# The last tiles of a graph gather cut into groups of 3, 2, 2 and 2 in place of 4, 3 and 2

## The chip, the cores and the metric

One core of one Trainium2 chip. The metric is the device time of one execution in microseconds (us), the median of several executions. Every execution does the whole computation once.

## The reference

The program is a small network on 6250 nodes with 256 features and 100000 edges sorted by destination. It has four layers, each added to its input: a graph layer that takes the mean over a node's neighbours, a mixture of eight experts of which each node takes two, a graph attention layer, and a second, smaller mixture. The change lies in the first layer and in the choice of experts of the second:

```python
x = x + _L0_gnn_ref(_layernorm(x, axis=-1), edge_index, L0_gnn_W, L0_gnn_b)
x = x + _L0_ffn_ref(_layernorm(x, axis=-1)[None], L0_ffn_Wg, ...)[0]
x = x + _L1_gnn_ref(_layernorm(x, axis=-1), edge_index, L1_gnn_W, L1_gnn_a_src, L1_gnn_a_dst)
x = x + _L1_ffn_ref(_layernorm(x, axis=-1)[None], L1_ffn_sW1, ...)[0]

# _L0_gnn_ref
neigh_sum = jax.ops.segment_sum(input_matrix[src], dst, num_segments=N_NODES)
neigh_mean = neigh_sum / jnp.maximum(deg, 1.0)[:, None]
out = jax.nn.relu(jnp.concatenate([input_matrix, neigh_mean], axis=-1) @ W + b)
return out / jnp.maximum(jnp.linalg.norm(out, axis=-1, keepdims=True), EPS)

# _L0_ffn_ref, the choice
gate_scores = jnp.einsum('bsd,ed->bse', x, Wg) + bg
topk_scores, topk_idx = jax.lax.top_k(gate_scores, K)
```

## The kernel before

Nodes lie in 49 tiles of 128 (`NT`; the last has 106 real nodes). Edges lie in 98 supers of 1024 (`NS`), each fetched by eight indirect DMAs of 128 rows that GpSimd issues one after the other (`gather_supers`, L699) into a ring of seven supers (`R0`); SyncE counts a super as landed at L851. A node tile's neighbour sum is made of items, one item for each pair of a super and a tile that meet in it: 146 in all (`ITEMS`). For an item VectorE builds a one-hot matrix (L712), TensorE multiplies it with the eight gathered blocks (L864), and VectorE adds the result to the tile's row of `ACC` (L1051).

The tiles are cut into groups by `GROUPS` (L43), and the work goes in rounds, an order that is written out by hand on each engine. Round r does the items of group r and then a tail in which four groups stand at four stages:

- group r (called new): divide by the degree (L1138, L1121), turn the rows (L876, L878), and the dense layer (L887, L889), with ScalarE copying and applying the relu (L963, L967, L973);
- group r-1 (mid): scale to unit length, add to `X` (L1125), moments (L1130, L196 to L204), normalise (L214), turn (L914) and the scores of the experts (L923);
- group r-2: on VectorE the best two experts (`choose`, L1060 to L1073), on TensorE their ranks (L904, L905), on VectorE the places in the experts' lists (`positions`, L1080 to L1101);
- group r-3 (old): tile by tile on VectorE three rows of hots for each of two choices (`list_hots`, L1110 to L1114), and on TensorE four products that write them into the lists (`to_lists`, L895).

So there are as many rounds as groups plus three (`LAGS`). TensorE and VectorE go through items and tail in program order, so no item is multiplied while a tail runs. The gather goes on beside it, as far as the ring lets it. VectorE's tail of a round:

```python
if new:
    ...
    tile_in(new[0], 0)
    tile_in(new[1], 1)
if 0 <= r - 2 < NG:
    choose(r - 2)
...
for n in range(max(len(new), steps, len(old))):
    if 2 <= n < len(new):
        tile_in(new[n], n)
    for t in mid[2 * n:2 * n + 2]:
        new_x(t)
    if n < len(old):
        list_hots(old[n], r - 3)
```

Items are taken in pairs, and the first pair of a group is read from a table that the kernel makes of the sorted edges (`tile_pair`, `group_span`). A third or fourth tile of a group enters its tail inside the loop, behind the hots of earlier steps. When the last round is over, all engines meet, and the experts' layer begins with the reading of the counts (L1241).

Of the kernel before, what the change touches and what calls it, by code (L numbers as in the profile page):

```python
# [27 lines left out]
class Sizes:  # L28


    def __init__(self, n_nodes, d, n_edges, n_exp, hid, heads):
        self.N, self.D, self.E = n_nodes, d, n_edges
        self.NT = -(-n_nodes // P)
        self.NPAD = self.NT * P
        self.KD = d // P
        self.Q = 8
        self.SE = self.Q * P
        self.NS = -(-n_edges // self.SE)
        self.RG = -(-self.NS * self.Q // P)
        self.EPAD = (self.RG * P + 1) * P  # L40
        self.R = 8
        self.R0 = 7
        self.GROUPS = (4,) * 11 + (3, 2)  # L43
        self.ECOLS = self.NT + self.NT % 2
        self.ITEMS = self.NS + self.NT - 1
        self.TABW = self.ITEMS + 4
        self.SRANGE = self.NS + 4
        self.BS = 2
        self.NB = self.NS // self.BS
        self.NE, self.HID = n_exp, hid  # L50
        self.KH = hid // P
        self.HEADS = heads
        self.TOK = 256
        self.ET = (2 * self.NPAD + n_exp * (self.TOK - 1)) // self.TOK
        self.LEAST = n_nodes * 2 // (8 * self.TOK) * 8
        self.NEVER = 8191
        assert self.ITEMS % 2 == 0 and self.NS % self.BS == 0 and self.R == 4 * self.BS and self.NB > 4
        assert self.NT % 2 and self.NEVER >= self.NPAD
        assert sum(self.GROUPS) == self.NT and min(self.GROUPS) >= 2 and self.NS % self.R0 == 0
        assert n_exp * self.ECOLS <= 512 and 2 * self.NT < 256  # L60
# [2417 lines left out]
```

How the kernel before makes its waits and increments, by code:

```python
    def settle(self):  # L73
        self.eng.wait_ge(self.sem, self.n)
# [110 lines left out]
        def ln_root(act, s_var, s_root):  # L185
            act.wait_ge(s_var, 1)
            nc.scalar.activation(lnt[:, 2], lnt[:, 0], ACT.Sqrt).then_inc(s_root, 1)
# [1 line left out]
        def ln_rstd(loc, s_root):  # L189
            loc.eng.wait_ge(s_root, 1)
            loc.link(nc.vector.reciprocal(rstd[:], lnt[:, 2]))
# [60 lines left out]
            def rows_ready(loc, s_rows, s_rowsf):  # L252
                loc.eng.wait_ge(s_rows, 16 * len(LISTS))
                loc.link(nc.vector.tensor_copy(rows_f[:], rows_i[:]))
                loc.link(nc.vector.tensor_tensor(rows_i[:, 0], rows_f[:, 1], rows_f[:, 2], ALU.is_gt))
# [16 lines left out]
            def store_gaps(sp, s_rowsf, s_gaps):  # L274
                sp.wait_ge(s_rowsf, 2)
                for n, to in enumerate((seg_gaps, gaps_back)):
                    sp.dma_start(to.rearrange("(g p e) -> p g e", p=P, e=P), gaps[:, n]).then_inc(s_gaps, 16)
                sp.wait_ge(s_gaps, 32)
# [1 line left out]
            def turn_lists(pe, s_rowsf, s_turned, s_copied):  # L280
                pe.wait_ge(s_rowsf, 1)
                for t in range(NTURN):
                    n, g = divmod(t, z.RG)
                    if t >= 2:
                        pe.wait_ge(s_copied, t - 1)
                    nc.tensor.matmul(pT[t % 2][:, 0:P], rows_f[:, n, g, :], front[:], start=True, stop=False)
                    nc.tensor.matmul(pT[t % 2][:, 0:P], rows_b[:, n, g, :], back[:], start=False, stop=True)\
                        .then_inc(s_turned, 1)
```

## Time and profile before

| what | before |
|---|---|
| median of 3 runs | 3563.06 us (3559.85 to 3564.49) |
| the profiled execution's own time | 3562.46 us |
| its span | 3560.7 us |
| first gather, GpSimd's DMAs | 103.6 to 1093.9 us of the span |
| tail of the last group begins (L1138) | 1119.6 us |
| next stage begins (L1241) | 1175.5 us |
| VectorE, TensorE busy | 50%, 78% |

The span runs from the first instruction to the last; the execution's own time is 1.8 us longer. Times in the trace's views are us from the span's start. A row of the timeline has start, length, engine, line, operation, the tiles written and read, how many instructions it merges, and in brackets how long the engine sat idle before it and for whom. PE is TensorE (PEld its weight loads), DVE VectorE, ACT ScalarE, POOL GpSimd, SP SyncE.

### The profile page before, as it was taken

Reading aid. Unit: us, or ns where it says so; the run is one execution under the profiler, and the core shown is the slowest. Engines: PE = TensorE matmul, PEld = TensorE weight load, DVE = VectorE, ACT = ScalarE, POOL = GpSimd, SP = SyncE. Lnnn points to the kernel's source line nnn. Section 1 sums busy time; section 2 is a strip of 40 time slices with the busy share of each in tenths; the row PEclk is TensorE's granted clock in tenths of the full one; section 3 lists DMA queues with packets and bytes.
Section 4 is the critical chain, followed back from the end, with each engine's and each line's share of the span. In section 5 each row is a group of like instructions: output and inputs, shape, how many; then the busy total and the mean of one; then the engine's idle time right before and its main releaser. Section 6 shows DMA issues by size and latency. Waiting matters only on the chain. (4 is left out here: it accounts for less than half of the span.)

```text
span 3560.7 us, 54707 instructions
## 1 busy us (share of the span) xinstructions
PE 2771.3 (78%) x12865; PEld 2282.5 (64%) x12866; DVE 1767.8 (50%) x4610; ACT 1149.8 (32%) x4236; POOL 1718.6 (48%) x1811
## 2 busy tenths in 40 slices
PE   1477778788887699999999445777777767768999
PEld 1356666666665488888888334555555555558888
DVE  5323455444456311111111656777777777766664
ACT  2000101000001122222222226556656556534554
POOL 0677777777772122222222037777777777500000
PEclk7688888888897799999999777888888887888999
DMA  4433333333331122212221544444444444300000
GB/s 148 124 105 111 110 109 110 114 112 109 110 110 46 71 85 81 91 60 89 100 70 59 159 123 112 110 109 110 110 110 109 110 110 110 86 23 14 17 19 21
DMA packets 157662, 328.30 MB, mean 92 GB/s; under 512 B 40129, under 2 KB 95323, under 8 KB 153356
## 3 DMA queue, kind: packets, MB, share of 16 engines
q0 software_dynamic: 85824, 236.38, 23.7%
q1 hardware_dynamic: 58816, 77.11, 6.4%
q10 hardware_dynamic: 12844, 12.82, 1.1%
q8 instruction: 65, 1.06, 0.1%
q14 instruction: 113, 0.93, 0.1%
HBM read 286.42 MB, written 41.86 MB: 92 GB/s over the span
## 5 line engine op out<-in xcount | busy, mean ns | idle before, releaser
L699 POOL DMA_INDIRECT G<-g_rows,srcT x784 | 742.3, 947 | 368.3 <-issue 236.7
L699 POOL DMA_INDIRECT G<-h_rows,srcT x784 | 752.8, 960 | 238.8 <-issue 237.6
L864 PE MATMUL pS<-G,O 128*128 x2336 | 565.9, 406 | 168.4 <-issue 98.2
L1789 PE MATMUL pS<-G,O 128*128 x2336 | 653.2, 446 | 37.5 <-issue 29.0
L864 PEld LDWEIGHTS pS<-G,O 128*128 128x128 f32 x2336 | 473.9, 205 | 256.8 <-issue 178.9
L1789 PEld LDWEIGHTS pS<-G,O 128*128 128x128 f32 x2336 | 507.0, 220 | 184.5 <-issue 59.1
L1858 ACT ACTIVATE G<-G 128x32 f32<-128x32 f32 x2352 | 503.1, 307 | 0.0
L1433 ACT ACTIVATE HE<-pH,b1s 128x256 f32<-128x256 f32 x432 | 204.9, 474 | 583.8 <-PE pH L1408 583.8
L1408 PE MATMUL pH<-XT,w1s 128*128 128x256 f32 x1728 | 384.5, 381 | 0.9 <-DVE XT L1448 0.9
L1418 PE MATMUL pY<-w2s,HE 128*128 128x256 f32 x1728 | 381.9, 379 | 0.0
L1340 POOL DMA_INDIRECT y_rows<-YE,yidx x108 | 109.3, 1012 | 527.7 <-DVE YE L1460 511.3
L1408 PEld LDWEIGHTS pH<-XT,w1s 128*128 128x128 f32 x1728 | 330.1, 191 | 46.6 <-issue 1.3
L1418 PEld LDWEIGHTS pY<-w2s,HE 128*128 128x128 f32 x1728 | 324.1, 190 | 41.8
L963 ACT ACTIVATE HT<-pT 128x512 f32<-128x512 f32 x49 | 29.2, 596 | 825.6 <-PE pT L878 825.5
L1799 PE MATMUL pA<-ident,SCO 128*64 128x128 f32 x196 | 52.0, 421 | 287.0 <-ACT SCO L1840 287.0
L1947 DVE SCALAR_TENSOR_TENSOR O<-iota_bank,tile_base,dstT 128x1024 f32<-128x1024 f32 x146 | 187.4, 1284 | 170.2 <-PE pS L1789 121.7
L712 DVE SCALAR_TENSOR_TENSOR O<-iota_bank,tile_base,dstT 128x1024 f32<-128x1024 f32 x149 | 191.2, 1284 | 130.8 <-issue 129.8
L1051 DVE TENSOR_TENSOR ACC<-ACC,pS 128x257 f32 x146 | 62.0, 424 | 318.8 <-PE pS L864 318.8
L1799 PEld LDWEIGHTS pA<-ident,SCO 128*64 128x64 f32 x196 | 26.3, 159 | 297.7 <-ACT SCO L1840 294.1
L1448 DVE COPY XT<-pX 128x512 f32<-128x512 f32 x55 | 38.1, 692 | 350.4 <-PE pX L1394 350.4
L1460 DVE TENSOR_TENSOR YE<-pY,b2s 128x256 f32<-128x256 f32 x108 | 40.8, 420 | 317.4 <-PE pY L1418 317.4
L2027 DVE TENSOR_TENSOR G<-G,pM 128x2560 f32<-128x2560 f32 x49 | 138.3, 2823 | 36.3 <-ACT pM L1852 34.2
(306 smaller groups left out, 3337.6 us busy)
## 6 DMA issues: line engine op xcount, KB each, us to landing
w1s<-in_W_dram SPq DMA_DIRECT2D x16, 1024.0 KB, 5.0
w2s<-in_W_dram SPq DMA_DIRECT2D x16, 1024.0 KB, 7.7
G<-h_rows,srcT POOLq DMA_INDIRECT x784, 2.8
Y<-y_rows SPq DMA_DIRECT2D x49, 256.0 KB, 4.3
G<-g_rows,srcT POOLq DMA_INDIRECT x784, 2.8
g_rows<-OUT SPq DMA_DIRECT2D x49, 132.0 KB, 2.5
h_rows<-ACC SPq DMA_DIRECT2D x7, 896.0 KB, 4.0
out_dram<-X SPq DMA_DIRECT2D x48, 128.0 KB
```

The source lines that it names most:

```text
L699: pool.indirect_dma_start(out=G[:, c % (ring * Q), 0:width], out_offset=None, in_=rows, in_offset=bass.IndirectOffsetOnAxis(ap=srcT[:, c:c ...
L712: return nc.vector.scalar_tensor_tensor(out=O[:, k], in0=iota_p[:].unsqueeze(1).to_broadcast([P, Q, P]), scalar=base, in1=dstT[:, bass.ds( ...
L864: mm = nc.tensor.matmul(pS[k][:, 0:W], O[:, k, q, :], G[:, bass.ds((s % R0) * Q + q, 1), :].rearrange("p a d -> p (a d)"), start=(q == 0), ...
L1340: pool.indirect_dma_start(out=y2_rows, in_=YE[:, k, h, :], in_offset=None, out_offset=bass.IndirectOffsetOnAxis(ap=yidx[:, k, h:h + 1], ax ...
L1408: mm = nc.tensor.matmul(pH[b % 3][:, 0:z.TOK], w1s[:, k, m, b * P:(b + 1) * P], XT[:, k, m, :], start=(m == 0), stop=(m == KD - 1))
L1418: mm = nc.tensor.matmul(pY[h][:, 0:D], HE[:, b, h * P:(h + 1) * P], w2s[:, k, b, :], start=(b == 0), stop=(b == KH - 1))
L1433: nc.scalar.activation(HE[:, b, :], pH[b % 3][:, 0:z.TOK], ACT.Relu, bias=b1s[:, k, b:b + 1]).then_inc(s_relu, 1)
L1789: mm = nc.tensor.matmul(pS[:, bass.ds((w % BANKS) * BANK, NR)], O[:, k, q, :], G[:, bass.ds((s % R) * Q + q, 1), 0:NR].rearrange("p a d -> ...
L1799: tr = nc.tensor.transpose(pA[0:64, j * P:(j + 1) * P], SCO[:, k % 2, j].rearrange("p f r -> p (f r)"), ident[:])
L1858: loc.tick(nc.scalar.activation(part[:, 0:HC], part[:, 0:HC], ACT.Copy, scale=part[:, HC:HW]))
L1947: nc.vector.scalar_tensor_tensor(out=O[:, k], in0=iota_p.unsqueeze(1).to_broadcast([P, Q, P]), scalar=tile_base[:, bass.ds(w0 + k + 2, 1)] ...
L2027: loc.tick(nc.vector.tensor_tensor(c[:, :, :, 0:HC], c[:, :, :, 0:HC], w.unsqueeze(3).to_broadcast([P, BC - SHARE, HEADS, HC]), ALU.mult))
```

## The change

One line. The groups end at tiles 40, 43, 45, 47 and 49, where they ended at 40, 44, 47 and 49; there are 14 groups for 13, and 17 rounds for 16. Groups 0 to 9 are as before.

```diff
-        self.GROUPS = (4,) * 11 + (3, 2)
+        self.GROUPS = (4,) * 10 + (3, 2, 2, 2)
```

The sorted edges of the reference, put through the kernel's rule for pairs, give the items of each group. Before: twelve for each group of four tiles, then 10 (items 132 to 141, three tiles) and 4 (142 to 145, two tiles). Now, from group 10 on: 8 (120 to 127), 6 (128 to 133), 8 (134 to 141) and 4 (142 to 145).

On TensorE, behind the score products of round 11 (L923, the last of a round's tail): the difference between the two orders, + now and - before. L821 and L822 read where a group's items begin and end.

```order
 L914 MATMUL pT<-ident,ACC 128x128 x2
 L923 MATMUL pZ<-Wg,HT 128x8 x4
-L895 MATMUL pL<-B,A 128x400 x16
+L821 TENSOR_LOAD tile_pair
+L821 ISA x2
+L822 TENSOR_LOAD tile_pair
```

Where the old last round ended in the lists of four tiles (16 products), another group's items now follow a tail with two new tiles.

On TensorE, the end of the stage, from the last score products of the last round with items: before,

```order
L923 MATMUL pZ<-Wg,HT 128x8 x4
L895 MATMUL pL<-B,A 128x400 x16
L904 MATMUL pS<-both,below 128x24
L905 MATMUL pS<-both,ones 128x24
L914 MATMUL pO<-ident,ACC 128x128 x2
L914 MATMUL pT<-ident,ACC 128x128 x2
L923 MATMUL pZ<-Wg,HT 128x8 x4
L895 MATMUL pL<-B,A 128x400 x12
L904 MATMUL pS<-both,below 128x16
L905 MATMUL pS<-both,ones 128x16
L895 MATMUL pL<-B,A 128x400 x8
```

and now:

```order
L923 MATMUL pZ<-Wg,HT 128x8 x4
L895 MATMUL pL<-B,A 128x400 x8
L904 MATMUL pS<-both,below 128x16
L905 MATMUL pS<-both,ones 128x16
L914 MATMUL pO<-ident,ACC 128x128 x2
L914 MATMUL pT<-ident,ACC 128x128 x2
L923 MATMUL pZ<-Wg,HT 128x8 x4
L895 MATMUL pL<-B,A 128x400 x8
L904 MATMUL pS<-both,below 128x16
L905 MATMUL pS<-both,ones 128x16
L895 MATMUL pL<-B,A 128x400 x8
```

The three rounds without items write the lists of 2, 2 and 2 tiles, where they wrote 4, 3 and 2. SyncE's and GpSimd's orders are the same in both.

## Rows read from the trace of the kernel before

**Rows 1.** Line L699 (the gather): operation and count, then who ended its waits (us, times).

```profile
L699 POOL DMA_INDIRECT G<-h_rows,srcT x784: 942/946/1242, 103.6 to 1093.9; - x196
...
  PE pS L864: 1.2, 4
```

**Rows 2.** Line L851 (SyncE counts a super as landed), and who waited for it.

```profile
L851 SPq EVENT_SEMAPHORE  x98: 17/17/17, 115.2 to 1097.3; - x98
...
  PE pS L864: 63.7, 16
```

**Rows 3.** Timeline, TensorE and VectorE, the first eight items of group 10.

```profile
955.35 36.92 PE L864 MATMUL pS<-G,O 128*128 x159 [2.82 <-issue]
...
985.68 0.43 DVE L1051 TENSOR_TENSOR ACC<-ACC,pS 128x257 f32 x1 [1.29 <-PE pS L864]
```

**Rows 4.** Timeline, tail of round 11 (3 new, 4 mid, 4 chosen, 4 old).

```profile
1074.20 0.17 DVE L1138 TENSOR_SCALAR rdeg<-ACC 128x3 f32<-128x3 f32 x1 [0.16 <-DVE ACC L1051]
...
1087.49 0.69 PE L876 MATMUL pT<-ident,IN 128*128 128x128 f32 x2 [4.45 <-DVE ACC L1121]
...
1088.40 3.62 PE L887 MATMUL pO<-W,HT 128*128 128x256 f32 x8
...
1093.38 0.35 DVE L1110 TENSOR_SCALAR A<-iota_n,slot,pcol 128x128 bf16<-128x128 f32 x1 [4.36 <-PE pL L895]
```

**Rows 5.** Timeline, the four items of group 12 (64 products) and their adds.

```profile
1103.07 15.80 PE L864 MATMUL pS<-G,O 128*128 x64 [2.67 <-issue]
...
1115.55 0.42 DVE L1051 TENSOR_TENSOR ACC<-ACC,pS 128x257 f32 x1 [0.93 <-PE pS L864]
...
1119.02 0.42 DVE L1051 TENSOR_TENSOR ACC<-ACC,pS 128x257 f32 x1 [1.30 <-PE pS L864]
```

**Rows 6.** Timeline, tail of round 12 (2 new, 3 mid, 4 chosen, 4 old).

```profile
1119.61 0.17 DVE L1138 TENSOR_SCALAR rdeg<-ACC 128x2 f32<-128x2 f32 x1 [0.16 <-DVE ACC L1051]
...
1122.60 1.89 PE L887 MATMUL pO<-W,HT 128*128 128x256 f32 x8
...
1127.28 1.51 PE L895 MATMUL pL<-B,A 128*128 128x400 bf16 x4 [2.57 <-DVE B L1114]
...
1127.80 0.47 DVE L1125 SCALAR_TENSOR_TENSOR X<-ACC,rnorm,X 128x256 f32<-128x256 f32 x1
...
1129.76 0.43 DVE L1130 BATCH_NORM_STATS2 stats<-X 128x6 f32<-128x256 f32 x1
...
1134.72 1.06 DVE L214 TENSOR_SCALAR ACC<-X,mean,rstd 128x256 f32<-128x256 f32 x3
...
1135.91 0.75 DVE L1080 TENSOR_TENSOR base<-base,pS 128x8 f32<-128x8 f32 x4
...
1137.32 1.25 PE L923 MATMUL pZ<-Wg,HT 128*128 128x8 f32 x8
...
1139.03 0.18 DVE L1060 TENSOR_TENSOR SC<-pZ,bg 128x24 f32<-128x24 f32 x1
```

**Rows 7.** Timeline, rounds 13 to 15 and the start of the next stage.

```profile
1146.76 0.35 DVE L1110 TENSOR_SCALAR A<-iota_n,slot,pcol 128x128 bf16<-128x128 f32 x1
...
1148.35 0.34 DVE L1110 TENSOR_SCALAR A<-iota_n,slot,pcol 128x128 bf16<-128x128 f32 x1
...
1156.92 0.17 DVE L1060 TENSOR_TENSOR SC<-pZ,bg 128x16 f32<-128x16 f32 x1
...
1167.08 0.36 DVE L1080 TENSOR_TENSOR base<-base,pS 128x8 f32<-128x8 f32 x2 [2.28 <-PE pS L905]
...
1175.51 0.21 DVE L1241 TENSOR_TENSOR dm<-mx 128x49 f32<-128x49 f32 x1 [2.61 <-PEq L116]
```

**Rows 8.** Windows (stretch, length, busy us by engine, granted TensorE clock): rounds 11 to 13.

```profile
1073.60:1103.10 29.50, 19.51 (x84) 13.50 (x84) 19.92 (x85) 6.20 (x18) 16.36 (x17) 0.77 0.37 97
1119.60:1138.60 19.00, 12.64 (x64) 8.63 (x64) 17.25 (x77) 4.26 (x13) 0.00 (x0) 0.91 0.01 3
1139.00:1156.90 17.90, 9.53 (x32) 5.25 (x32) 14.77 (x69) 0.97 (x3) 0.00 (x0) 0.54 0.07 25
```

## The prediction

> **What bounds the kernel now.** The page says that TensorE is busy 78% of the span and VectorE 50%, but that is a mean over stages, so I read the first layer alone: first the gather's line, then SyncE's landing line, then the timeline of the last two rounds with items, then the rounds behind them. The gather is 784 DMAs from 103.6 to 1093.9 us and waited for TensorE only 1.2 us in all [rows 1]: GpSimd sets the pace, and the ring never filled for long. TensorE waited 63.7 us for landed supers, 16 times [rows 2]; that is the slack of the early rounds. The last super is counted at 1097.3 [rows 2], while the last four items begin at 1103.07 [rows 5]. So at the end TensorE is already 6 us behind the gather, and the program's order decides: items, tail, items, tail, each engine in turn. From 1119.61 no items are left, and what follows until 1175.51 [rows 6, 7] is 55.9 us of tails alone, in which the groups still under way run out.
>
> The change therefore moves two sums against each other: the time until the last item is added, where a further tail is put in, and the time behind it, where smaller groups run out sooner. Both are worked out from the profiled execution (3562.46 us, 0.6 us under the median of 3563.06).
>
> **Until the last item, before.** Group 10's items begin at 955.35 [rows 3] and the last group's tail begins at 1119.61 [rows 6]: 164.3 us.
>
> **Until the last item, now.** Groups 0 to 9 are untouched, so group 10 begins at the same time. Seven steps follow.
>
> 1. Group 10 has 8 items. The eighth add starts at 985.68 [rows 3], and a tail begins 0.6 us behind the start of the last add (1119.02 to 1119.61, [rows 5, 6]): 986.3, so 30.9 us. These eight were multiplied without a wait for the gather in the trace, at one per 3.48 us (1115.55 to 1119.02, [rows 5]).
> 2. The tail of round 10 now has 3 new, 4 mid, 4 chosen and 4 old tiles, just as round 11 had: 1074.20 to the next group's first product at 1103.07 [rows 4, 5], 28.9 us.
> 3. Group 11 has 6 items. The last group's four took 1103.07 to 1119.61, 16.5 us [rows 5, 6]; two more at 3.48 us make 23.5 us.
> 4. The tail of round 11 has 2 new, 3 mid, 4 chosen, 4 old, as round 12 had: from 1119.61 to the end of the last score product, 1137.32 + 1.25 = 1138.57 [rows 6], 19.0 us, and 2.7 us until a next item's product (the idle time before 1103.07, [rows 5]): 21.7 us. It is shorter than 28.9 because both new tiles come ahead of the loop. In the longer tail the third is late: TensorE waits 4.45 us for it, and then VectorE 4.36 us for TensorE [rows 4].
> 5. Group 12 has 8 items: 16.5 + 4 x 3.48 = 30.4 us.
> 6. The tail of round 12 is step 4 with one mid tile less. That takes from VectorE one L1125 (0.4 us), one L1130 (0.4 us) and a third of the three L214 (0.35 us) [rows 6], 1.2 us in all: 20.5 us.
> 7. Group 13 has the same four last items: 16.5 us.
>
> The sum is 30.9 + 28.9 + 23.5 + 21.7 + 30.4 + 20.5 + 16.5 = 172.4 us, **8.1 us more** than 164.3. No step waits for the gather: the last items begin at 955.35 + 155.9 = 1111.3, and all supers are in by 1097.3 [rows 2]. Nor does the ring hold the gather up so that it counts: even a few us of delay would end before 1111.
>
> **Behind the last item.** Before: 19.4 us for round 12 (1119.61 to 1139.03), 17.9 for round 13 (to 1156.92), and the rest [rows 6, 7]. VectorE is busy 17.25 of the 19.0 us and 14.77 of 17.9 [rows 8], so its work is the path. An old tile costs it 1.6 us (1146.76 to 1148.35, [rows 7]). The four last rounds now stand against the old four:
>
> - first: one mid tile less (1.2 us), one old less (1.6), two prefix adds less (L1080 takes 0.75 us for four and 0.36 for two, [rows 6, 7]): 3.2 us;
> - second: two old less (3.2), one prefix add and a little of `choose` less (0.3): 3.5 us;
> - third: one old tile less: 1.6 us;
> - fourth: the same.
>
> That is **8.3 us less**. The number of instructions of `choose` and `positions` per round stays, and these cost nearly the same for two tiles as for three (0.17 against 0.18 us for L1060, [rows 6, 7]); their extra round is within the 8.1.
>
> **Everything else.** The stores of the normalised rows are 14 for 13 with the same bytes, issued by ScalarE, which idles in the tails; I take nothing for them. Later stages only start earlier or later.
>
> The balance is 8.1 - 8.3 = -0.2 us: **no change**, 3562.3 us on the profiled execution, and 3562.9 beside the median. The unknown that the sum leans on is the two-tile tail in the middle of the gather, which the trace shows only once and at the end. Its ends are 19.0 us (round 12 with no gap behind it) and 28.9 us (the three-tile tail, [rows 4, 5]), twice; I take 21.7 and 20.5, since the same counts of tiles stand in round 12 and only a clock can change them.
>
> Here a rule speaks against the change. The row shows a small VectorE operation at 0.17 us for two tiles and 0.18 us for three [rows 6, 7]. The Trainium skill, Perfetto Trace Analysis, Optimizing Scalar/DVE Operations, says that Scalar and DVE operations carry a fixed overhead each and that grouping into larger ones improves throughput where the engine is saturated; by that alone the sum would keep the 8.1 us of the extra round. The trace agrees on the fixed cost. The same section allows the opposite where the engine is not saturated but makes others wait, and here both hold in turn.
>
> **Rivals.**
>
> *The new tails run at the low clock (slower).* In round 12's tail the granted clock was 0.91, in round 11's 0.77 and in round 13's 0.54 [rows 8], between the levels 1.2 and 2.4 GHz; the dense step of a tile took 1.89 us at the higher and 3.62 us at the lower [rows 4, 6]. If the clock is low while a new tile's dense step runs, TensorE ends later than VectorE. Its 2.57 us of waiting for VectorE [rows 6] cover the first tile's 1.7 us; the second tile's 1.7 us and some 1.3 us of its list and score products are left. That is 3 us a tail in the three tails with two new tiles, 9 us together: 3571.9. It decides once the clock is below about 0.7 in them. For it speaks round 11's 0.77; against it that items run just before, as before round 12. By the Trainium skill, TensorE: Matmul & The Clock Gate, HAM oscillation, bursts between waits pay for a cold start each time; the windows agree that tails lower the clock.
>
> *The end is not shortened (slower).* If in the last rounds TensorE's chain of lists, ranks and scores ends behind VectorE's, the tiles taken away free VectorE only to wait. With half of the 8.3 us lost it is 3567.0, with all of it 3571.2. Against it: VectorE's busy share there; for it, 2.28 us of waiting for the ranks in round 14 [rows 7], and the clock of 0.54.
>
> *The further tail is hidden (faster).* If the last group still began at 1103, its gather being the limit, the 8.3 us would be pure gain: 3554.6. It needs the seven steps to be 8 us shorter. For it speaks only that the gather, too, ends at 1097.3; against it that six of seven steps repeat rows.
>
> **How the numbers follow.** A measurement of this kernel tells from no change about 0.2%, 7.1 us. The forecast has 0.68, with 5 us either way (3558 to 3568). The low clock has 0.12, nearly all beyond 7.1 us. The end not shortened has 0.12, mostly within 7.1 us, 0.02 beyond. The hidden tail has 0.08. So faster 0.08, same 0.78, slower 0.14. The range that leaves out less than 2 in 10 runs from 3557 to 3571.
>
> **What would show it.** In the changed profile: four L1138 rows at about 986, 1039, 1091 and 1128 us; 8, 6, 8 and 4 items between the tails; no wait for SyncE's L851 behind group 10; the next stage (L1241) at 1175 instead of 1175.5, 47.5 us behind the last L1138. The prediction is wrong if that start lies more than 7 us from 1175.5, or if the two sums are off and only cancel.

## The result: 0.16% faster, and not where the change was made

| | before | after |
|---|---|---|
| median of 20 runs each | 3561.69 us (3556.65 to 3567.61) | 3557.66 us (3553.52 to 3560.23) |
| ratio | 1 | 0.9984, 95% interval 0.9978 to 0.9990 |
| the profiled execution's own time | 3562.46 us | 3557.87 us |
| its span | 3560.7 us | 3556.1 us |
| last group's tail begins (L1138) | 1119.6 us | 1130.0 us |
| next stage begins (L1241) | 1175.5 us | 1177.6 us |
| last stage's first product (L2162) | 3165.0 us | 3166.1 us |
| last stage, from that product to the end | 395.7 us | 390.0 us |

The time lies inside the forecast range and 5 us under its centre. The change is smaller than the 0.2% that the prediction took as the least a measurement can tell, but 20 runs a side resolve it: it is a gain, and the forecast had no reason for one. (The ratio weighs all runs; that of the two medians is 0.9989. Its interval stands for 3.6 to 7.8 us.) The last two rows of the table hold the gain. The program arrives at its last stage 1.1 us later than before and then runs that stage, whose code is the same to the letter, 5.7 us faster.

The first layer first. The gather and the landing line of the kernel after, which answer to [rows 1, 2]:

```profile
L699 POOL DMA_INDIRECT G<-h_rows,srcT x784: 942/946/1262, 102.7 to 1090.8; - x196
...
  PE pS L864: 0.9, 3
```

```profile
L851 SPq EVENT_SEMAPHORE  x98: 17/17/17, 114.4 to 1094.2; - x98
...
  PE pS L864: 65.9, 15
```

The gather is as it was, and TensorE waits for it as long as before. The timeline of the kernel after, VectorE's four L1138 that open the tails and TensorE's items between them, with the start of the next stage (they answer to the firsts and lasts of [rows 3 to 7]):

```profile
953.12 30.15 PE L864 MATMUL pS<-G,O 128*128 x128 [2.66 <-issue]
...
984.01 0.17 DVE L1138 TENSOR_SCALAR rdeg<-ACC 128x3 f32<-128x3 f32 x1 [0.16 <-DVE ACC L1051]
...
1012.69 24.12 PE L864 MATMUL pS<-G,O 128*128 x96 [2.70 <-issue]
...
1037.54 0.22 DVE L1138 TENSOR_SCALAR rdeg<-ACC 128x2 f32<-128x2 f32 x1 [0.16 <-DVE ACC L1051]
...
1061.40 30.62 PE L864 MATMUL pS<-G,O 128*128 x128 [2.29 <-issue]
...
1092.75 0.17 DVE L1138 TENSOR_SCALAR rdeg<-ACC 128x2 f32<-128x2 f32 x1 [0.16 <-DVE ACC L1051]
...
1112.35 16.89 PE L864 MATMUL pS<-G,O 128*128 x64 [2.05 <-issue]
...
1129.97 0.17 DVE L1138 TENSOR_SCALAR rdeg<-ACC 128x2 f32<-128x2 f32 x1 [0.16 <-DVE ACC L1051]
...
1177.59 0.21 DVE L1241 TENSOR_TENSOR dm<-mx 128x49 f32<-128x49 f32 x1 [2.61 <-PEq L116]
```

Items of 8, 6, 8 and 4 stand between the tails (96 products are 6 items, 128 are 8, 64 are 4), TensorE waits for no super (L851) between 984 and 1130 us, and the end behind the last L1138 is 1177.59 - 1129.97 = 47.6 us, where it was 55.9. So the change does what it says, and it is nearly a draw: from the first gather to L1241 it takes 1177.59 - 102.7 = 1074.9 us, and took 1175.51 - 103.6 = 1071.9, so it is 3.0 us longer in this pair of profiles. From L1241 to the last stage it is 1988.5 us and was 1989.5.

Now the last stage. In it each round of tiles is added to its input and normalised on VectorE (L2314 to L214), turned and multiplied on TensorE (L2162 to L2208). Two starts differ first, some 39 us into the stage. The timeline of the kernel before, VectorE at L2314 and TensorE's next burst:

```profile
3203.74 0.16 DVE L2375 TENSOR_TENSOR pr<-mx 128x4 f32<-128x4 f32 x1
3204.05 0.42 DVE L2314 TENSOR_TENSOR T<-ACC,RS 128x256 f32<-128x256 f32 x1
...
3208.41 0.69 PE L2162 MATMUL pT<-ident,IN 128*128 128x128 f32 x2 [8.76 <-DVE IN L214]
...
3213.12 1.92 PE L2179 MATMUL pS<-ACC,sW 128*128 128x128 f32 x8
3214.83 2.43 PE L2184 MATMUL pE<-ACC,eW 128*128 128x128 f32 x16
```

and of the kernel after, the same instructions:

```profile
3204.77 0.16 DVE L2375 TENSOR_TENSOR pr<-mx 128x4 f32<-128x4 f32 x1
3205.44 0.43 DVE L2314 TENSOR_TENSOR T<-ACC,RS 128x256 f32<-128x256 f32 x1 [0.51 <-DVE pr L2375]
...
3209.79 0.69 PE L2162 MATMUL pT<-ident,IN 128*128 128x128 f32 x2 [9.12 <-DVE IN L214]
...
3214.06 1.06 PE L2179 MATMUL pS<-ACC,sW 128*128 128x128 f32 x8
3214.95 1.95 PE L2184 MATMUL pE<-ACC,eW 128*128 128x128 f32 x16
```

VectorE stands 0.51 us ahead of L2314, where in the kernel before it stood 3204.05 - 3203.74 - 0.16 = 0.15 us; counted from the stage's first product, L2314 starts at 39.02 us before and at 39.37 after. TensorE's burst (its next run of products, from L2162 on) starts 0.34 us later with it (43.38 and 43.72). And then the later burst overtakes: its eight L2179 take 1.06 us in place of 1.92. The windows (stretch, length, busy us and count of PE, PEld, DVE, ACT, POOL, then the granted TensorE clock, the DMA share and GB/s) say why. Before, the idle time, the first 3.9 us of the burst, the 3.5 us behind them, and two places later in the stage:

```profile
3202.10:3208.40 6.30, 0.00 (x0) 0.00 (x0) 5.32 (x28) 1.70 (x3) 0.00 (x0) 0.51 0.02 5
3208.40:3212.30 3.90, 3.89 (x17) 3.34 (x17) 3.83 (x12) 1.16 (x4) 0.00 (x0) 0.50 0.02 4
3212.30:3215.80 3.50, 3.50 (x18) 3.50 (x18) 1.11 (x4) 1.73 (x6) 0.00 (x0) 0.50 0.00 0
...
3295.00:3303.00 8.00, 6.68 (x39) 5.83 (x38) 5.09 (x19) 3.77 (x14) 0.00 (x0) 0.79 0.05 16
3449.00:3459.00 10.00, 8.67 (x52) 7.64 (x51) 7.54 (x31) 3.77 (x14) 0.00 (x0) 0.83 0.05 15
```

and after, the same five places:

```profile
3203.20:3209.70 6.50, 0.00 (x0) 0.00 (x0) 5.17 (x28) 1.70 (x3) 0.00 (x0) 0.51 0.01 3
3209.80:3213.50 3.70, 3.70 (x16) 3.15 (x16) 3.63 (x12) 0.98 (x3) 0.00 (x0) 0.50 0.00 0
3213.50:3216.90 3.40, 3.40 (x33) 3.40 (x32) 1.29 (x4) 1.79 (x7) 0.00 (x0) 0.99 0.00 0
...
3296.10:3304.10 8.00, 8.00 (x60) 7.18 (x58) 5.67 (x18) 4.48 (x16) 0.00 (x0) 1.00 0.06 19
3450.10:3460.10 10.00, 9.25 (x68) 8.39 (x69) 6.74 (x19) 6.29 (x24) 0.00 (x0) 1.00 0.09 28
```

In the idle time the granted clock falls to its lower level, 1.2 GHz. Before, it stays there through the third row (0.50, 18 products); after, it is back at 2.4 GHz (0.99, 33 products). By the trace's clock record the low stretch began 37.15 us into the stage before and 37.24 after, and ended at 50.80 and at 47.48. Two later low stretches of the kernel before, 132.7 and 289.7 us into the stage, are gone (the last two rows). The stage spends 44.1 us at the low clock before and 31.6 after, its start and end included. By ScalarE's starts, the lead over the kernel before grows at just these places: it is 1.4 us at 55 us of the stage, 2.3 at 106 (the low stretch between them lies 3.3 us earlier), 3.9 at 137 and 5.7 at 305.

### The profile page after: what moved, and what is told of

The parts are those of the page before. It is cut to its first block and busy times, and to the rows that moved or that the text cites. A ratio compares the mean times of both kernels' runs of the same rounds, so it can differ in the third digit from the quotient of the medians.

```text
span 3556.1 us, 54778 instructions
## 1 busy us (share of the span) xinstructions
PE 2763.5 (78%) x12869; PEld 2277.8 (64%) x12870; DVE 1773.1 (50%) x4648; ACT 1148.1 (32%) x4238; POOL 1716.1 (48%) x1811
## 5 line engine op out<-in xcount | busy, mean ns | idle before, releaser
L699 POOL DMA_INDIRECT G<-g_rows,srcT x784 | 741.9, 946 | 368.0 <-issue 237.7
L699 POOL DMA_INDIRECT G<-h_rows,srcT x784 | 750.6, 957 | 238.8 <-issue 237.9
L712 DVE SCALAR_TENSOR_TENSOR O<-iota_bank,tile_base,dstT 128x1024 f32<-128x1024 f32 x149 | 191.2, 1283 | 133.7 <-issue 132.7
```

Of the source, the lines that this page charges most:

```text
L699: pool.indirect_dma_start(out=G[:, c % (ring * Q), 0:width], out_offset=None, in_=rows, in_offset=bass.IndirectOffsetOnAxis(ap=srcT[:, c:c ...
L712: return nc.vector.scalar_tensor_tensor(out=O[:, k], in0=iota_p[:].unsqueeze(1).to_broadcast([P, Q, P]), scalar=base, in1=dstT[:, bass.ds( ...
```

## The experiments

Two theories. **Draw and clock:** in the first layer the two sums cancel as forecast, and all the gain comes from the 0.35 us delay of L2314, which turns the low stretch's end. **First layer:** the new groups do save time there, and the last stage's difference is chance. Each kernel was timed in 11 or 12 runs beside runs of the kernel before on the same chip. Stage times are those of each one's profiled execution. In the diffs only changed lines stand; the lines that set up the tiles `pad` (80 columns, in pad_83 96) and `late_by` are left out.

**Both kernels again, unchanged.** Does the difference belong to the programs or to one execution?

> The kernel before, unchanged, to see how far two runs of one program differ, in the total and stage by stage. Both theories: ratio 1.000, within 0.1%. Theory 'clock of the last stage is chance': the stretch from the last stage's start (3165 us) to the end, 395.6 us in the first trace with 45.4 us at the low clock, comes out different by several us here, since only where TensorE's clock falls changed. Theory 'the change shortens the last stage': it stays within 1 us of 395.6 us.

> The change, unchanged, a second time. Theory 'chance': the ratio moves toward 1.000 or above (the first layer of its first trace is 3.0 us longer from the first gather to the next stage), and the last stage is not again 5.6 us shorter. Theory 'real': the ratio is again 0.998 to 0.999 and the gain stands in the same stage of its new trace.

Before again: 3561.75 us, ratio 1.0000 (0.9991 to 1.0009), last stage 395.7 us. After again: 3557.95 us, ratio 0.9988 (0.9979 to 0.9997), last stage 390.0 us. To a tenth of a microsecond, the last stage repeats in a second execution of each program, so it isn't chance. The first layer does not repeat so well: from the gather to L1241 the change took 1070.1 us this time, against 1074.9 in its first profile, and the kernel before 1071.5 against 1071.9. Nor are the stages between untouched: from L1241 to the last stage the change is 1.1 us shorter in both pairs, which no run explains; with the old groups and other small edits this stretch took from 1987.1 (nudge) to 1989.5 us (before).

**Other groups.** Is it this grouping, any further round, or any new order?

early_pair, more_twos and swap_342, in this order, each in place of the old line:

```diff
+        self.GROUPS = (2, 2) + (4,) * 10 + (3, 2)
+        self.GROUPS = (4,) * 9 + (3, 2, 2, 2, 2, 2)
+        self.GROUPS = (4,) * 10 + (3, 4, 2)
```

> Groups of 2 and 2 at the start in place of the first 4, the end as before (3, 2): one round and as many instructions more as the change has, but the extra tail where TensorE waits for the gather anyway, and the run-out unchanged. Theory 'the groups at the end make the time': first layer as before within 1 us, ratio 1.000 within 0.05%. Theory 'what comes with one more round (program length, shifted code) changes later stages': ratio 0.998 to 0.999 as with the change, with the gain behind the first layer.

> Groups end with 3, 2, 2, 2, 2, 2 behind nine of four: two more rounds than the change, the same run-out. Theory 'the rounds' own sums': two more tails at the end put the last group's tail some 6 to 7 us later than in the change, the run-out stays at 47.6 us, so the first layer ends about 8 us later than before and the total is 3 us (0.1%) slower than before, or 6 us slower than the change. Theory 'smaller groups gain by more rounds': the total falls by another 4 us or more below the change.

> Groups end with 3, 4 and 2 where before they end with 4, 3 and 2: as many groups, rounds and instructions as before, in another order. So far the last stage took 395.7 us in both traces of before and 390.0 us in all four of programs with a round more. Theory 'more instructions ahead of it change the last stage': it stays at 395.7 us here. Theory 'any change of the first layer moves it': 390.0 us. The first layer's end moves by 2 us or less either way; ratio 1.000 within 0.1% by the first theory, 0.9985 by the second.

| | ratio (95%) | L2314 at | last stage |
|---|---|---|---|
| early_pair | 0.9990 (0.9981 to 0.9999) | 39.38 | 390.0 us |
| more_twos | 0.9986 (0.9977 to 0.9995) | 39.06 | 389.9 us |
| swap_342 | 1.0011 (1.0002 to 1.0020) | 39.02 | 395.7 us |

early_pair settles much. It has the further round at the front, and its end is the old one (57.7 us from the last L1138 to L1241, 55.9 before), so none of the predicted saving is in it; it gains all the same, and by the same 5.7 us in the last stage. swap_342 has as many rounds as before, keeps the slow last stage, and is a little slower (in its profile, 1075.2 us from the gather to L1241; that is beyond the 2 us expected). So the gain goes with the number of rounds, and not with small groups at the end. more_twos has 15 groups, one round more than the change and not two as its expectation says. Both theories there missed: it is neither slower than before nor 4 us faster than the change. It was a surprise in another way too: fast stage, though L2314 is only 0.04 us late. More on that below.

**Time without rounds.** Does it need only that the first layer's code be longer or later?

The first two lines are pad_dve, the last two pad_pe; pad_all has both, and three activations of one column on ScalarE.

```diff
+                    for n in range(75):
+                        nc.vector.memset(pad[:, n:n + 1], 0.0)
...
+                    for _ in range(27):
+                        nc.tensor.matmul(pO[:, 0:D], ones_b[:], b3[:], start=True, stop=True)
```

They stand ahead of the first items, and what they write is not read.

> The kernel before with 75 memsets of one column on VectorE ahead of the first gather's items, as many instructions as the change adds there, while VectorE waits for the first super anyway; groups as before. Theory 'more VectorE instructions change the last stage': last stage 390.0 us, first layer as before within 2 us (its clock varies by that), ratio 0.9985. Theory 'the groups are needed': last stage 395.7 us, ratio 1.000.

> The kernel before with 27 small products (54 instructions on TensorE; the change adds 55) ahead of the first items; groups as before. Theory 'more TensorE instructions change the last stage': last stage 390.0 us and ratio 0.9985. If only VectorE's count matters: 395.7 us and 1.000.

> The kernel before with both pads that had no effect alone, 75 memsets on VectorE and 27 products on TensorE, and three activations of one column on ScalarE: as many instructions as the change adds on each engine; groups as before. Theory 'program length on all engines together moves the last stage': 390.0 us and ratio 0.9985. Theory 'the further round itself does (its place in time, its store)': 395.7 us and 1.000.

Nothing moved: 0.9997 (0.9987 to 1.0006), 0.9999 (0.9990 to 1.0008) and 1.0003 (0.9995 to 1.0012), L2314 at 38.99 to 39.03 us, last stage 395.6 to 395.7. The paddings were meant to be as long as the round's code. pad_dve was 8 instructions short of it, which came out only later; until then these runs spoke against code length as the cause.

**The delay alone.** Old groups, and a memset on VectorE right ahead of that one L2314, of 1 column (nudge) or of 320 (nudge_more):

```diff
+                                if r == 2 and s == 3:
+                                    nc.vector.memset(late_by[:], 0.0)
```

> The kernel before with one memset of one column on VectorE in the last stage, just ahead of the product at L2314 that starts 39.02 us into it in both traces of before, and 0.35 us later in three of the four shorter ones. Theory 'a fraction of a us there decides how long TensorE's clock stays low': last stage 390.0 us, and all 5.7 us of gain with the first layer untouched, ratio 0.9985. Theory 'the cause lies ahead of the last stage': 395.7 us and 1.000.

> The kernel before with a memset of 320 columns on VectorE at the same place of the last stage as the memset of one column, which cost no time there (the product at L2314 again began at 39.03). Groups as before. In the change, L2314 begins 0.35 us later than before and the products behind TensorE's wait at 43.7 us and not 43.38; the granted clock is back at 47.4 us and not 50.8. Theory 'that delay alone decides': L2314 0.3 to 0.4 us later, clock back at 47.4, last stage 390 us, ratio 0.9985 with the first layer as before. Theory 'the delay is a bystander': last stage 395.7 us or more, ratio 1.000.

The one column fitted into the gap ahead of L2314 (39.03 us) and did nothing: 0.9993 (0.9984 to 1.0002), last stage 396.0. The 320 columns delay it to 39.34. The timeline of nudge_more (its lines are 2 higher):

```profile
3201.95 0.16 DVE L2377 TENSOR_TENSOR pr<-mx 128x4 f32<-128x4 f32 x1
3202.35 0.33 DVE L2414 MEMSET late_by<- 128x320 f32 x1 [0.24 <-DVE pr L2377]
3202.59 0.36 DVE L2316 TENSOR_TENSOR T<-ACC,RS 128x256 f32<-128x256 f32 x1
...
3206.89 0.69 PE L2164 MATMUL pT<-ident,IN 128*128 128x128 f32 x2 [9.03 <-DVE IN L214]
...
3211.20 1.06 PE L2181 MATMUL pS<-ACC,sW 128*128 128x128 f32 x8
3212.09 1.95 PE L2186 MATMUL pE<-ACC,eW 128*128 128x128 f32 x16
```

The eight products of the burst are at 1.06 us, the last stage takes 390.4 us, and the kernel 3555.72 us, ratio 0.9988 (0.9979 to 0.9996). An added instruction that makes VectorE later brings what the change brought, with the old groups. That shows the delay to be a sufficient cause; the memset of one column, an added instruction without a delay, is its control. It is also the lowest median of the study, though it can't be told apart from the change.

**The low stretch taken away.** Unread products keep TensorE busy in two rounds of the last stage, in the old groups (busy_before) and in the new (busy_after). If the clock is all, the two should be equal.

```diff
+                            for _ in range({3: 34, 4: 10}.get(r, 0)):
+                                nc.tensor.matmul(pS2[:, 256:256 + P], ident[:], ident[:], start=True, stop=True)
```

> The kernel before with products on TensorE whose results nobody reads, in the last stage: 34 where it waits 8.8 us for VectorE (ahead of the fourth group's first turn), 10 where it waits 2.8 us. Theory 'the clock after these waits is what the last stage's two times differ by': TensorE stays at the high clock there, the low stretch of 44.1 us in this stage falls to 25 us or less and the stage to 390 us or below. Theory 'VectorE sets the pace there and the clock only follows': 395 us or more.

> The change with the same unread products in the last stage. Theory 'the change's gain is the clock of the last stage alone': this takes as long in the last stage as the same products on the kernel before, within 1 us, and the two totals differ by the first layer alone, that is by 0 to 3 us in favour of the old groups. Theory 'the groups gain by themselves': 4 to 6 us less in total than the kernel before with the same products.

The windows of busy_before and then of busy_after, where the low stretch was:

```profile
3201.00:3211.20 10.20, 9.04 (x79) 8.55 (x78) 9.17 (x39) 4.26 (x12) 0.00 (x0) 1.00 0.00 0
3204.60:3214.80 10.20, 8.68 (x76) 8.19 (x75) 8.80 (x38) 3.89 (x11) 0.00 (x0) 1.00 0.01 3
```

The low stretch at 37 us is gone in both (granted clock 1.00), and the last stage takes 392.2 and 392.3 us, although L2314 starts at 38.99 in one and 39.37 in the other. The kernels measured 3558.66 (0.9993, 0.9984 to 1.0001) and 3559.49 us (0.9991, 0.9983 to 1.0000). Both bounds of the first expectation were missed (390 us or below, 395 or more): low stretches at 81.6, 129.4 and 286.4 us are left, the same in both. With the clock made equal, nothing of the difference between the groups is left that these runs could show.

**Why a further round delays L2314.** The trace shows no other engine that holds it up: the code waits at L2314 only for VectorE's own additions, and the profile puts the idle time down to VectorE's own L2375. But in after, a_again, early_pair and busy_after a transfer of the queue that the page lists as "q14 instruction" starts 40.0 to 40.1 us into the stage, 0.7 us behind the delayed L2314. In before, swap_342 and pad_pe it stands at 22 us (with the next at 72), in pad_dve at 40.3, in pad_all at 40.6. It is not moved by TensorE's padding and is moved by VectorE's, so it follows how long VectorE's code is. It is a sign and not the delay itself: it starts behind the stall, and in pad_dve it stands at 40.3 us without one. Counted in the traces, the further round adds 83 instructions to VectorE's code: 52 that are run, and one more copy of the loop over a group's items, whose 31 instructions are run no more often in all; pad_dve had 75. So: 83 of them on the old groups, and, the other way, 40 of them on the new groups, to move the place away again.

pad_83, and behind the line of dots what after_pad40 adds to the change:

```diff
+                    for n in range(83):
+                        nc.vector.memset(pad[:, n:n + 1], 0.0)
...
+                    for n in range(40):
+                        nc.vector.memset(pad[:, n:n + 1], 0.0)
```

> Old groups, and 83 memsets of one column on VectorE ahead of the first items, where the further round adds 83 instructions to VectorE's code (pad_dve had 75). Theory, VectorE's place in its code decides: a DMA of the instruction queue starts about 40.1 us into the last stage, L2314 starts at 39.37 us in place of 39.0, the last stage takes 390.0 us, and the ratio is about 0.9985. Rival, the further round delays L2314 by something else (its data, its stores, its waits): L2314 at 39.0, last stage 395.7 us, ratio 0.9995 to 1.0010.

> The change's groups, and 40 memsets of one column on VectorE ahead of the first items. Theory, VectorE's place in its code decides: the instruction DMA moves away from 40.1 us into the last stage, the stall ahead of L2314 goes (39.0 us), the last stage takes 395.7 us again, and the ratio is 0.9995 to 1.0010, so the change gains nothing. Rival, the further round itself causes the delay: stall and 390.0 us stay, ratio about 0.9988.

The timeline of pad_83, old groups (its lines here are 3 higher):

```profile
3207.68 0.16 DVE L2378 TENSOR_TENSOR pr<-mx 128x4 f32<-128x4 f32 x1
3208.34 0.42 DVE L2317 TENSOR_TENSOR T<-ACC,RS 128x256 f32<-128x256 f32 x1 [0.50 <-DVE pr L2378]
...
3212.71 0.69 PE L2165 MATMUL pT<-ident,IN 128*128 128x128 f32 x2 [9.12 <-DVE IN L214]
...
3216.93 1.06 PE L2182 MATMUL pS<-ACC,sW 128*128 128x128 f32 x8
```

It is the row of the kernel after, but for a hundredth: 0.50 us of standing, a wait of 9.12 us, 1.06 us for the eight products. L2314 is at 39.38 us, the instruction transfer at 40.1, the last stage takes 390.0 us, and the kernel 3557.65 us, ratio 0.9985 (0.9976 to 0.9994). Eighty-three instructions of no use, run some 3 ms earlier, do what the change did; seventy-five don't. (pad_83's chip has no profile of the kernel before; its total there, 3561.05 us, is the usual one.)

The timeline of after_pad40, the change's groups:

```profile
3205.20 0.16 DVE L2378 TENSOR_TENSOR pr<-mx 128x4 f32<-128x4 f32 x1
3205.51 0.43 DVE L2317 TENSOR_TENSOR T<-ACC,RS 128x256 f32<-128x256 f32 x1 [0.15 <-DVE pr L2378]
...
3209.87 0.69 PE L2165 MATMUL pT<-ident,IN 128*128 128x128 f32 x2 [8.77 <-DVE IN L214]
...
3214.15 1.06 PE L2182 MATMUL pS<-ACC,sW 128*128 128x128 f32 x8
```

The delay is gone, as expected (39.03 us; the transfer is at 28.1), and the kernel with the change's groups measures 0.9995 (0.9986 to 1.0004): its gain can't be told from none, nor from the rival's 0.9988. So it is the trace that speaks against the rival here, by the stall. And the expectation missed the last stage. It was to be 395.7 us and is 391.8; the burst starts as early as in the kernel before and is fast all the same, and of the two later low stretches only that at 286 us has come back. Here the low stretch itself had begun earlier, at 36.93 us and not at 37.2.

That, and more_twos, fit one pattern, found afterwards and set by no run of its own. What divides all 14 profiles that have this low stretch is not when the burst starts, but how far behind the low stretch's start:

| | burst behind the start of the low stretch | low stretch ends at | last stage |
|---|---|---|---|
| before, b_again, swap_342, three pads, nudge | 6.11 to 6.23 us | 50.8 to 50.9 us | 395.6 to 396.0 us |
| more_twos | 6.27 us | 47.4 us | 389.9 us |
| after_pad40 | 6.46 us | 47.2 us | 391.8 us |
| after, a_again, early_pair, nudge_more, pad_83 | 6.39 to 6.59 us | 47.4 to 47.5 us | 390.0 to 390.4 us |

In these profiles 6.23 us goes with the longer stretch and 6.27 with the shorter, less than a tenth of a microsecond apart.

## Why the prediction was right and wrong

**Until the last item: +8.1 us forecast, +12.6, +8.9 and +12.4 measured** (after against before, a_again against b_again, the busy pair). The steps are the right ones; the size was too small. From the starts in the profile after and in that of a_again:

| step | forecast | after | a_again |
|---|---|---|---|
| 1, eight items | 30.9 | 30.9 | 30.6 |
| 2, tail with three new | 28.9 | 28.7 | 28.6 |
| 3, six items | 23.5 | 24.9 | 24.7 |
| 4, tail with two new | 21.7 | 23.9 | 22.1 |
| 5, eight items | 30.4 | 31.4 | 30.5 |
| 6, tail with two new | 20.5 | 19.6 | 19.4 |
| 7, four items | 16.5 | 17.6 | 17.3 |
| sum | 172.4 | 176.9 | 173.2 |

The two-tile tails in the middle of the gather, on which the forecast leaned, cost 19.4 to 23.9 us, within the ends of 19.0 and 28.9. The windows of the three tails after,

```profile
984.00:1012.70 28.70, 17.04 (x84) 11.91 (x84) 19.80 (x84) 6.20 (x18) 21.76 (x23) 0.81 0.41 119
1037.50:1061.40 23.90, 16.51 (x65) 11.53 (x65) 17.94 (x79) 4.42 (x13) 18.35 (x19) 0.68 0.41 117
1092.80:1112.40 19.60, 11.95 (x59) 8.32 (x59) 16.21 (x75) 4.05 (x12) 0.00 (x0) 0.88 0.07 24
```

and the second of them in a_again,

```profile
1037.00:1059.00 22.00, 15.41 (x64) 10.38 (x64) 18.35 (x80) 4.26 (x13) 16.82 (x18) 0.77 0.42 122
```

show what varies: the granted clock of 0.68 in one execution and 0.77 in the other. That is the first rival in small, at the point from which it was said to decide (0.7): 2.2 us over the forecast in one tail of one execution, and 0.4 us in a_again, while the rival asked for 3 us in each of three tails. But of the 4.5 us that after is over the sum, the tails hold only 1.1; the items of steps 3, 5 and 7 hold 3.4. They too go with the clock: the last four items took 16.5 us at a granted clock of 0.90 before, 17.6 at 0.85 in after and 17.3 at 0.86 in a_again. The forecast had taken their time from the row at 0.90; for the eight items of step 5 it had 30.4 us, though its own step 1 has 30.9.

**Behind the last item: right, -8.3 us.** 47.6 us forecast, 47.6 and 47.5 measured. The rival that the end is not shortened is refuted.

**The balance: within the 5 us allowed, but not the -0.2 us forecast.** From the start of group 10 to L1241 it was +4.3, +0.5 and +4.2 us in the three pairs of profiles. From the first gather it was +3.0 us in the first and 1070.1 - 1071.5 = -1.4 in the second, because the stretch ahead of group 10, which the change leaves as it was, came out 1.3 and 1.8 us shorter there. The medians of the busy pair differ by +0.8 us. The signs that the prediction named hold: the four L1138 lie within 2.3 us of its steps, and L1241 at 1177.6 is 2.1 us from 1175.5, where it allowed 7. The rival of a hidden further tail gave 3554.6 us, not far from the time measured, but for the wrong reason: the last L1138 came 10.4 us later than before, not at the same time.

**"Everything else ... Later stages only start earlier or later": this step failed.** The prediction took a stage with the same code to last the same time. It gave no reason for that. In place of 0 the last stage measured -5.7 us in the first pair of profiles and -5.6 in the second. The whole measured gain is about that size (0.16% of 3562 us is 5.7; the medians differ by 4.0). Its parts, each tried by itself: a further round makes VectorE's code 83 instructions longer; so VectorE stands 0.35 us longer ahead of L2314 in the last stage (pad_83 brings it with the old groups, after_pad40 takes it away with the new); so TensorE's burst starts later behind the clock's fall, and the low stretch is 3.4 us shorter (10.24 us for 13.65; nudge_more brings that by hand, the busy pair takes the low stretch away in both). Not every shorter last stage comes that way: more_twos and after_pad40 have no stall. The theory that the new groups save time where they stand has fallen with early_pair and pad_83.

Could it have been foreseen? The row of an 8.76 us wait ahead of a burst at the low clock stood in the trace of before. Its sign did not: the prediction could only have said that any shift of a few tenths in the last stage may be worth several microseconds either way, and have widened "same" for it.

**Open.** Why VectorE stands when its code has that length was not tried further; the trace shows only that an instruction transfer starts 0.7 us later. Nor was it tried why the low stretch began 0.25 us sooner in after_pad40, of which there is one profile, nor why 6.23 and 6.27 us lie on two sides.

## What to carry to other kernels

When a change gains a few tenths of a per cent, compare the stages that it does not touch before crediting it: here the gain lay 2 ms behind it. A useful control is a padding with as many instructions as the change adds, counted exactly, since 75 in place of 83 gave the opposite answer. A gain of this kind can go away with the next edit: 40 unrelated instructions removed the stall, and the total could no longer be told from that of the old groups; that a burst behind a long wait is cheap or dear by a tenth of a microsecond is a reason to shorten the wait, not to tune its length.

## What the runs showed of the hardware

- **Code length acts at a distance.** 83 added instructions on VectorE, ahead of the first layer's items, make the same engine stand 0.35 us longer some 3 ms later, and 75 don't. The transfer of the instruction queue moved from 22 to 40.1 us of the last stage with the 83, and to 40.3 with the 75.
- **The clock's pattern can belong to the program.** In the last stage the low stretch began at 37.15 to 37.24 us in 13 of 14 profiles, and the stage's time repeated within 0.1 us, while in the first layer two executions of one program differed by 5 us. The Trainium skill, TensorE: Matmul & The Clock Gate, What's actually happening, says that the count of products at the low clock varies from run to run of one kernel. The trace agrees in the first layer, where one tail had a granted clock of 0.68 in one execution and 0.77 in another, and not in the last stage; there the measurement decides.
- **A later burst can be done sooner.** TensorE's burst that starts 0.34 us later has its eight L2179 done at 3214.06 + 1.06 = 3215.1, 49.0 us into the stage, against 3213.12 + 1.92 = 3215.0, 50.0 us into it, before.
